# A four-layer graph and expert network on one core: 68 of 400 count scatters sent in two earlier stages, and the dense experts' bias rows weighted by VectorE

## The chip, the core and the metric

The kernel runs on one core of a Trainium2 chip. The metric is device time in microseconds (us) from the first to the last instruction of one execution; several executions are taken and the median is told.

## What is computed

The reference runs four layers, each a graph block and a feed-forward block, each on the layer-normed node features `x` (3125 nodes, 256 features) and each added back to `x`. There are 50000 edges with `src`, `dst` (sorted) and 64 edge features. Only two of the eight blocks matter here.

```python
# layer 0, feed-forward: 8 dense experts, all of them for every node
w   = softmax(xn @ Wr + br)                        # [3125, 8]
h1  = relu(scale1[e] * (xn @ W1[e]) + shift1[e])   # batch norm folded
h2  = relu(scale2[e] * (h1 @ W2[e]) + shift2[e])
x  += sum_e w[:, e] * (h2 @ Wo[e] + bo[e])
# layer 1, graph, three rounds of mean aggregation over the in-edges
h   = relu(mean_{edges into n} h[src] @ Wl + bl + h @ Wr + ...)
```

The bias row `bo[e]` enters each node as `sum_e w[n, e] * bo[e]`. The mean over in-edges is taken with a matrix of edge counts (node by node), which has to be built once from the list of edges.

## The kernel before

Nodes lie in 25 tiles of 128 rows, five tiles to a chunk (`CH`), 640 rows a chunk (`TOK`). The program is a sequence of stages. Each stage is a `Phase` with one `Block`: every engine (PE = TensorE, DVE = VectorE, ACT = ScalarE, POOL = GpSimd, SP = SyncE) runs its own hand-written list, with semaphores between them, and at the end all engines meet at a barrier. So the next stage starts when the slowest engine of the stage is through.

Around the change the stages are, in order:

- `edge_logits` (L692) of the first graph block. It gathers a row for each edge slot, and beside that writes zeros over the count matrix in DRAM (`counts`, L752, ACT's queue, semaphore `g.filled`) and works out on DVE, from all pairs of columns of the edge list, where each count goes (`put_at`) and how large it is (`put_n`).
- `segment_max` (L859): the maximum of the logits over each node's edges, by transposes on PE and four long scans on DVE. POOL has nothing here.
- `bulk`, then `edge_sum` (L576), in which POOL multiplies messages, then `bulk` again.
- `ffn0` (L1411): `node_rows` (L373) makes layer norm, the transposed rows `xt` and the router's logits; POOL has nothing here. `bulk` makes the softmax and folds the batch norms. `turn_weights` (L1166) transposes the router weights `w` into `wt`, 8 x 3200. `experts` (L1196) runs the dense experts.
- `gnn1` (L1724), whose first stage is `node_rows` again. Its last stage, `mean_layers` (L964), is the first that reads `counts`.

`experts` loops five times over the chunks. Within one iteration the order of the layers is fixed by a skewed list: expert e's first layer, expert e-1's second, expert e-2's output. Inner products go to `ps_h` (four buffers) and ACT makes the next hidden rows of them (L1307). Output products go to `ps_y` (four buffers); DVE multiplies each by the expert's weight, a column of `wc`, and adds it to `y` (L1325 for expert 0, L1327 for the others). After expert 7 come five more products a chunk, `wtc` (8 x 128, turned weights) with `b_out` (8 x 256), which are the weighted bias rows (L1280); DVE adds them with L1329. Then DVE adds `y` to `x` (L1333), and copies the next chunk's weights (L1316). PE may be four output products ahead of DVE:

```python
pe.wait_ge(added, i * NO + max(n - 3, 0))
```

Beside all this POOL sends the 400 scatters that put the counts into DRAM (L1244), one for each column of 125 edges, and lets at most 40 (`BK`) stand open before it waits for them. It first waits for `g.filled`. It waits for all 400 before the stage may end:

```python
pool.wait_ge(put, 16 * EC)
```

SP loads `b_out` and then the experts' weights, 24 loads of 256 KB; expert 0 starts when its three are there.

Of the kernel before, what the change touches and what calls it, by code (L numbers as in the profile page):

```python
# [6 lines left out]
ALU = mybir.AluOpType  # L7
ACT = mybir.ActivationFunctionType
# [31 lines left out]
BK = 40  # L40
CN = NT * P
# [312 lines left out]

def by_partition(ap):

    return ap.rearrange("(k p) c -> p k c", p=P)
# [15 lines left out]
def node_rows(nc, g, srcs, w_drams, cols, bias, sinks, ln=False, xn=None, xt=None, relu_add=None):  # L373
# [7 lines left out]
    with Phase(nc) as ph:  # L381
# [29 lines left out]
        with nc.Block() as block:  # L411
            @block.sync
# [446 lines left out]
def segment_max(nc, g, logits, maxima, H):  # L859
# [6 lines left out]
    with Phase(nc) as ph:  # L866
# [299 lines left out]
def turn_weights(nc, g, wts, wts_t):  # L1166

    with Phase(nc) as ph:
        fixed = ph.sb("fixed", [P, CH, NE], F32)
        ps_w = ph.ps("ps_w", [P, 2, 512])  # L1170
        laid, turned, taken = ph.sem("laid"), ph.sem("turned"), ph.sem("taken")
        with nc.Block() as block:
            @block.vector
            def _(dve):
                with nc.vector.Fori(0, NT // CH) as i:
                    dve.wait_ge(turned, i)
                    nc.vector.tensor_copy(fixed[:], wts[:, ds(i * CH, CH), :]).then_inc(laid, 1)

            @block.tensor
            def _(pe):  # L1180
                with nc.tensor.Fori(0, NT // CH) as i:
                    pe.wait_ge(laid, i + 1)
                    pe.wait_ge(taken, i * 2)
                    for j in range(CH):
                        ins = nc.tensor.transpose(ps_w[0:NE, j // 4, (j % 4) * P:(j % 4 + 1) * P], fixed[:, j, :], g.ident[:])
                    ins.then_inc(turned, 1)

            @block.scalar
            def _(act):
                with nc.scalar.Fori(0, NT // CH) as i:  # L1190
                    act.wait_ge(turned, i + 1)
                    nc.scalar.activation(wts_t[:, ds(i * TOK, 512)], ps_w[0:NE, 0, :], ACT.Copy).then_inc(taken, 1)
                    nc.scalar.activation(wts_t[:, ds(i * TOK + 512, P)], ps_w[0:NE, 1, 0:P], ACT.Copy).then_inc(taken, 1)


def experts(nc, g, xt, hidden, w_last, b_last, wts, wts_t):  # L1196
# [11 lines left out]
    outer = [(e, t) for e, l in order if l == L for t in range(CH)] + [(NE, t) for t in range(CH)]  # L1208
# [4 lines left out]
    with Phase(nc) as ph:  # L1213
# [3 lines left out]
        b_out = sb("b_out", [NE, D], F32)  # L1217
        wc = sb("wc", [P, CH, NE], F32)
        wtc = sb("wtc", [NE, TOK], F32)
# [4 lines left out]
        b_in, made, shaped, made_y, added, stored, wc_in, wt_in, put = (sem(x) for x in (  # L1224
            "b_in", "made", "shaped", "made_y", "added", "stored", "wc_in", "wt_in", "put"))
        with nc.Block() as block:
            @block.sync
            def _(sp):
                sp.dma_start(b_out[:], b_last).then_inc(b_in, 16)
# [7 lines left out]
            @block.gpsimd  # L1237
            def _(pool):
                pool.wait_ge(g.filled, 16 * ((NT + 1) * CH + ES))
                for b in range(EC // BK):  # L1240
                    if b:
                        pool.wait_ge(put, 16 * BK * b)
                    for j in range(b * BK, (b + 1) * BK):
                        nc.gpsimd.indirect_dma_start(  # L1244
                            out=g.counts, out_offset=bass.IndirectOffsetOnAxis(ap=g.put_at[:, j:j + 1], axis=0),
                            in_=g.put_n[:, j:j + 1], in_offset=None).then_inc(put, 16)
                pool.wait_ge(put, 16 * EC)

            @block.tensor
            def _(pe):  # L1250
                with nc.tensor.Fori(0, NT // CH) as i:
# [17 lines left out]
                    def outer_layer(e):  # L1269
                        if e < NE:  # L1270
                            pe.wait_ge(shaped, i * NI + done[(e, L - 1)])
                        else:
                            pe.wait_ge(wt_in, i + 1)
                            pe.wait_ge(b_in, 16)
                        for t in range(CH):
                            n = out_at[(e, t)]
                            pe.wait_ge(added, i * NO + max(n - 3, 0))
                            if e == NE:

                                ins = nc.tensor.matmul(ps_y[:, n % 4, 0:D], wtc[:, t * P:(t + 1) * P], b_out[:],  # L1280
                                                       start=True, stop=True)
                            else:
                                K = dims[L] // P
                                for k in range(K):
                                    ins = nc.tensor.matmul(ps_y[:, n % 4, 0:D], hid[L - 1][:, e % 2, k, t * P:(t + 1) * P],
                                                           ws[L][:, e, k, :], start=k == 0, stop=k == K - 1)
# [7 lines left out]
                    outer_layer(NE)  # L1294

            @block.scalar
            def _(act):
                with nc.scalar.Fori(0, NT // CH) as i:
                    act.wait_ge(made_y, i * NO)
# [1187 lines left out]
```

## Time and profile before

| | us |
|---|---|
| median of 3 runs | 7201.81 (7201.0 to 7206.65) |
| profiled execution, its own time | 7212.82 |
| its span, first to last instruction | 7211.0 |
| `segment_max` of the first graph block | 725.9 to 784.7 |
| `node_rows` of `ffn0` | 1069.7 to 1105.4 |
| `turn_weights` with both barriers | 1115.1 to 1127.8 |
| `experts`, to the next stage's first instruction | 1127.8 to 1763.7 |

Stages are given in us from the span's start. A row of the timeline has start, length, engine, line, operation, output <- input, and, in brackets, how long the engine was idle before it and what ended that. Rows that follow one another on an engine with the same names are merged (x5 are five instructions in one row). "SPq" is SP's queue of transfers, of which the row shows the issue and not the landing.

### The profile page before, as it was taken

How to read it: one execution, taken by the hardware profiler on the slowest of the kernel's cores; microseconds unless marked ns; L12 is line 12 of the kernel's file. 1: busy time of each engine (PE TensorE's matmuls, PEld its weight loads, DVE VectorE, ACT ScalarE, POOL GpSimd, SP SyncE). 2: the span in 40 equal slices, each digit the busy share in tenths (PEclk: the TensorE clock that was granted, in tenths of full speed). 3: DMA queues.
4: the chain of work that ended last, by engine and by line, in shares of the span. 5: the costliest groups of instructions: out<-in, count | busy, mean ns of one | idle time of the engine just before them, and what ended most of it. 6: DMA issues, size and time to landing. Idle time of an engine off the chain costs nothing. (4 is left out here: it accounts for less than half of the span.)

```text
span 7211.0 us, 90552 instructions
## 1 busy us (share of the span) xinstructions
PE 5064.2 (70%) x22571; PEld 4059.3 (56%) x22572; DVE 3026.6 (42%) x7105; ACT 1493.2 (21%) x3806; POOL 3390.5 (47%) x3180
## 2 busy tenths in 40 slices
PE   2877578995655487999994823329465886888466
PEld 2777456773344365888884723326354665766344
DVE  5655672222443472101011131137614775677453
ACT  1000563331000380000002310009231221222121
POOL 1777465775477480000003237748333776677100
PEclk8555788997877798999996955559687998899687
DMA  2999451001699563444544548857263886788100
GB/s 76 353 344 318 146 169 37 1 1 17 228 337 335 194 222 95 125 127 125 139 117 151 179 116 236 236 161 236 86 194 108 263 262 198 230 264 264 43 0 22
DMA packets 831975, 1217.80 MB, mean 169 GB/s; under 512 B 120484, under 2 KB 617741, under 8 KB 831785
## 3 DMA queue, kind: packets, MB, share of 16 engines
q1 hardware_dynamic: 386617, 514.07, 24.2%
q0 software_dynamic: 143680, 378.88, 18.0%
q10 hardware_dynamic: 301488, 322.74, 12.7%
q8 instruction: 67, 1.10, 0.1%
q14 instruction: 123, 1.01, 0.0%
HBM read 840.14 MB, written 374.71 MB: 168 GB/s over the span
## 5 line engine op out<-in xcount | busy, mean ns | idle before, releaser
L570 POOL DMA_INDIRECT logit_rows<-tab,src_a x832 | 824.7, 991 | 340.9 <-issue 229.0
L570 POOL DMA_INDIRECT max_rows<-tab,src_a x832 | 786.6, 945 | 382.4 <-issue 236.1
L689 PE MATMUL ps_a<-msg,sel 128*128 128x264 f32 (+2 forms) x2496 | 625.3, 399 | 124.3 <-DVEq L621 67.9
L1565 POOL DMA_INDIRECT moe_x<-xn,slot x100 | 97.2, 972 | 1218.3 <-POOLq L93 1188.4
L689 PEld LDWEIGHTS ps_a<-msg,sel 128*128 128x128 f32 x2496 | 453.4, 191 | 296.1 <-DVE acc L635 98.3
L1244 POOL DMA_INDIRECT counts<-put_n,put_at x400 | 476.6, 1192 | 251.1 <-issue 235.8
L1055 PE MATMUL ps_a<-hl,blocks 128*128 128x256 f32 x2600 | 578.0, 379 | 0.5 <-PE ps_a L1055 0.3
L1055 PEld LDWEIGHTS ps_a<-hl,blocks 128*128 128x128 f32 x2600 | 491.9, 190 | 78.1 <-issue 13.6
L570 POOL DMA_INDIRECT logit_rows<-tab_kv,src_a x416 | 397.6, 956 | 241.2 <-issue 117.7
L2004 DVE TENSOR_TENSOR_SCAN run<-same,run,ps_t 128x512 f32<-128x512 bf16 x416 | 508.4, 1265 | 0.9 <-PE ps_t L1932 0.9
L600 POOL TENSOR_TENSOR msg<-edge_rows,extra 128x1024 f32<-128x1024 f32 x208 | 393.4, 1904 | 200.6 <-DMA edge_rows<-slot_rows 126.0
L1923 PE MATMUL ps_e<-w,att 64*128 64x256 f32 x1664 | 467.2, 426 | 22.2 <-DMA att<-in_attr_t 22.2
L851 PE MATMUL ps_b<-q,sel_t 128*128 x832 | 303.0, 529 | 232.9 <-DVE sel_t L770 232.9
L851 PE MATMUL ps_b<-cols,sel_t 128*128 x832 | 194.4, 363 | 369.2 <-DVE sel_t L770 369.1
L1974 ACT ACTIVATE back<-ps_b 128x512 f32<-128x512 f32 x416 | 229.0, 595 | 850.0 <-PE ps_b L1941 822.0
L660 ACT ACTIVATE far<-lane,loc_a 128x128 f32<-128x128 f32 x1248 | 398.5, 390 | 16.9 <-PEq L93 6.9
L851 PEld LDWEIGHTS ps_b<-cols,sel_t 128*128 128x128 f32 x832 | 185.2, 328 | 378.7 <-issue 378.6
L1995 DVE TENSOR_TENSOR msg<-max_rows,ps_e 128x512 f32<-128x512 f32 x416 | 274.2, 685 | 292.3 <-DMA max_rows<-tab,src_a 184.5
L851 PEld LDWEIGHTS ps_b<-q,sel_t 128*128 128x128 f32 x832 | 209.7, 264 | 326.3 <-issue 288.3
L1121 DVE SCALAR_TENSOR_TENSOR new<-ps_a,rdeg,acc 128x256 f32<-128x256 f32 x75 | 36.2, 483 | 845.1 <-PE ps_a L1066 845.1
L1923 PEld LDWEIGHTS ps_e<-w,att 64*128 64x128 f32 x1664 | 327.1, 207 | 111.2 <-issue 60.3
L925 ACT ACTIVATE lt<-ps_x 128x512 f32<-128x512 f32 (+3 forms) x12 | 6.4, 552 | 1750.7 <-PE ps_x L899 1750.7
(439 smaller groups left out, 9409.0 us busy)
## 6 DMA issues: line engine op xcount, KB each, us to landing
slot_rows<-logit_rows ACTq DMA_DIRECT2D x312, 512.0 KB
edge_rows<-slot_rows SPq DMA_DIRECT2D x312, 512.0 KB
blocks<-counts SPq DMA_DIRECT2D x390, 320.0 KB
seg_rows<-back ACTq DMA_DIRECT2D x208, 512.0 KB
counts<-zeros ACTq DMA_DIRECT2D x130, 320.0 KB
locs<-loc_slots SPq DMA_DIRECT2D x312, 128.0 KB
att<-in_attr_t SPq DMA_DIRECT2D x1248, 32.0 KB
wf<-in_L_ffn_W SPq DMA_DIRECT2D x57, 512.0 KB
```

The lines of the kernel that those rows point to most:

```text
L570: self.nc.gpsimd.indirect_dma_start(out=self.rows[:, (n % Q) * Q + j, :], out_offset=None, in_=table, in_offset=bass.IndirectOffsetOnAxis( ...
L600: nc.gpsimd.tensor_tensor(msg[:, b % 2, :, 0:D].rearrange("p j (h d) -> p j h d", h=heads), ring.rows[:, b * Q:(b + 1) * Q, :].rearrange(" ...
L660: ins = nc.scalar.activation(far[:, n % 2, j, :], g.lane[:], ACT.Abs, scale=-1.0, bias=g.loc_a[:, n * Q + j:n * Q + j + 1])
L689: nc.tensor.matmul(ps_a[:, n % 8, 0:C], sel[:, b % 2, j, :], rhs, start=True, stop=True).then_inc(summed, 1)
L851: ins = nc.tensor.matmul(product(b, j), sel_t[:, b % 2, j, :], node_cols[:, ds(tiles[j], 1), :].rearrange("p a c -> p (a c)"), start=True, ...
L1055: ins = nc.tensor.matmul(ps_a[:, q % 2, 0:D], blocks[:, k % RC, n % CH, :], sides[l][:, n, :], start=n == 0, stop=i == 0 and n == NT - 1)
L1244: nc.gpsimd.indirect_dma_start(out=g.counts, out_offset=bass.IndirectOffsetOnAxis(ap=g.put_at[:, j:j + 1], axis=0), in_=g.put_n[:, j:j + 1 ...
L1565: nc.gpsimd.indirect_dma_start(out=g.moe_x, out_offset=bass.IndirectOffsetOnAxis(ap=slot[:, c, t:t + 1], axis=0), in_=xn[:, t, :], in_offs ...
L1923: ins = t.matmul(ps_e[:, k, j * D:(j + 1) * D], att[:, b * Q + 2 * k + j, :], w[:], start=True, stop=True)
L1974: a.activation(back[:, s:s + 2, :].rearrange("p j d -> p (j d)"), ps_b[:, k, :], ACT.Copy).then_inc(taken, 1)
L1995: v.tensor_tensor(msg[:, s:s + 2, :], ring.rows[:, s:s + 2, :], ps_e[:, k, :].rearrange("p (j d) -> p j d", j=2), ALU.add).then_inc(mixed, 1)
L2004: v.tensor_tensor_scan(run[:, b, c, :], same[:, b, :], ps_t[:, b % 2, c, :], run[:, (b - 1) % Q, c, GP - 1:GP], ALU.mult, ALU.max).then_in ...
```

## The change

1. The loop of scatters becomes a function `put_counts(nc, g, pool, lo, hi)` that sends columns lo to hi. `segment_max` of the first graph block sends 40 of them, `node_rows` of `ffn0` 28, `experts` the other 332. The wait for `g.filled` moves with the first, the wait for all 400 stays in `experts`. The semaphore is now one of the whole program.
2. `turn_weights` is gone, and with it `wt`, `wtc` and ACT's copy of `wtc` at the start of each iteration.
3. `b_out` now holds all eight bias rows on each of the 128 partitions (a broadcast load of 128 x 2048 in place of 8 x 256), and stands ahead of the weights on SP's queue as before. At the start of each iteration DVE builds `y` of the weighted bias rows: 5 `tensor_scalar`, then 35 `scalar_tensor_tensor`, all of them SBUF to SBUF. All output products are then added with `scalar_tensor_tensor`. The five bias products and five additions at the end of the iteration are gone.

```diff
+PUT0, PUT1 = 40, 68
+def put_counts(nc, g, pool, lo, hi):
+    if lo == 0:
+        pool.wait_ge(g.filled, 16 * ((NT + 1) * CH + ES))
+    for j in range(lo, hi):
+        if j and j % BK == 0:
+            pool.wait_ge(g.put, 16 * j)
+        nc.gpsimd.indirect_dma_start(
+            out=g.counts, out_offset=bass.IndirectOffsetOnAxis(ap=g.put_at[:, j:j + 1], axis=0),
+            in_=g.put_n[:, j:j + 1], in_offset=None).then_inc(g.put, 16)
+    if hi == EC:
+        pool.wait_ge(g.put, 16 * EC)
...
-def node_rows(nc, g, srcs, w_drams, cols, bias, sinks, ln=False, xn=None, xt=None, relu_add=None):
+def node_rows(nc, g, srcs, w_drams, cols, bias, sinks, ln=False, xn=None, xt=None, relu_add=None, puts=(0, 0)):
...
+            if puts[1]:
+                @block.gpsimd
+                def _(pool):
+                    put_counts(nc, g, pool, *puts)
...
-def segment_max(nc, g, logits, maxima, H):
+def segment_max(nc, g, logits, maxima, H, puts=(0, 0)):
...
+            if puts[1]:
+                @block.gpsimd
+                def _(pool):
+                    put_counts(nc, g, pool, *puts)
...
-def experts(nc, g, xt, hidden, w_last, b_last, wts, wts_t):
+def experts(nc, g, xt, hidden, w_last, b_last, wts):
...
-    outer = [(e, t) for e, l in order if l == L for t in range(CH)] + [(NE, t) for t in range(CH)]
+    outer = [(e, t) for e, l in order if l == L for t in range(CH)]
...
-        b_out = sb("b_out", [NE, D], F32)
+        b_out = sb("b_out", [P, NE, D], F32)
...
-                sp.dma_start(b_out[:], b_last).then_inc(b_in, 16)
+                sp.dma_start(b_out[:].rearrange("p e d -> p (e d)"), row_bc(b_last.rearrange("e d -> (e d)"))).then_inc(b_in, 16)
...
-                    for j in range(b * BK, (b + 1) * BK):
-                        nc.gpsimd.indirect_dma_start(
...
+                put_counts(nc, g, pool, PUT1, EC)
...
-                            if e == NE:
-                                ins = nc.tensor.matmul(ps_y[:, n % 4, 0:D], wtc[:, t * P:(t + 1) * P], b_out[:],
-                                                       start=True, stop=True)
...
-                    nc.scalar.activation(wtc[:], wts_t[:, ds(i * TOK, TOK)], ACT.Copy).then_inc(wt_in, 1)
...
+                dve.wait_ge(b_in, 16)
                 with nc.vector.Fori(0, NT // CH) as i:
...
+                    for e in range(NE):
+                        for t in range(CH):
+                            if e == 0:
+                                ins = v.tensor_scalar(y[:, t, :], b_out[:, 0, :], wc[:, t, 0:1], None, ALU.mult)
+                            else:
+                                dve.wait_ge(based, i * NO + e * CH + t - CH + 1)
+                                ins = v.scalar_tensor_tensor(y[:, t, :], b_out[:, e, :], wc[:, t, e:e + 1], y[:, t, :], ALU.mult, ALU.add)
+                            ins.then_inc(based, 1)
...
-            segment_max(nc, g, logits, maxima, 8)
+            segment_max(nc, g, logits, maxima, 8, puts=(0, PUT0))
...
+        node_rows(nc, g, [g.x], [(g.ins["L0_ffn_Wr"], 0, 0)], NE, g.ins["L0_ffn_br"], [(0, NE, w, None)], ln=True, xt=xt, puts=(PUT0, PUT1))
...
-        turn_weights(nc, g, w, wt)
```

The order on three engines shows it. On POOL, from the last gathers of the first `edge_logits` to the next `edge_logits`, before (`msg` is the messages of `edge_sum`, the ISA rows are the barriers):

```order
L570 DMA logit_rows<-tab,src_a 128x264 x416
L721 UNCONDITIONAL_BRANCH
L92 ISA x3
L592 UNCONDITIONAL_BRANCH
L600 TENSOR_TENSOR msg<-edge_rows,logits 128x4x256 x104
L591 UNCONDITIONAL_BRANCH
L92 ISA x5
L1237 UNCONDITIONAL_BRANCH
L1244 DMA counts<-put_n,put_at 10654720x1 x400
```

and now:

```order
L905 UNCONDITIONAL_BRANCH
L363 DMA counts<-put_n,put_at 10654720x1 x40
L903 UNCONDITIONAL_BRANCH
L93 ISA x2
L612 UNCONDITIONAL_BRANCH
L620 TENSOR_TENSOR msg<-edge_rows,logits 128x4x256 x104
L611 UNCONDITIONAL_BRANCH
L93 ISA x2
L428 UNCONDITIONAL_BRANCH
L363 DMA counts<-put_n,put_at 10654720x1 x28
L426 UNCONDITIONAL_BRANCH
L93 ISA x2
```

Forty scatters now stand ahead of the messages, 28 behind them, and one barrier fewer follows. The other 332 come after the last row shown.

On DVE, from `turn_weights` to the start of the experts' loop, before (`fixed` is a chunk of the router weights for the transpose):

```order
L1177 ISA
L1177 COPY fixed<-w 128x40
L1175 REGISTER_ALU
L1175 COMPARE_AND_BRANCH
L1172 UNCONDITIONAL_BRANCH
L1311 UNCONDITIONAL_BRANCH
L1314 UNCONDITIONAL_BRANCH
L1314 ISA
L1316 ISA
L1316 COPY wc<-w 128x40
L1317 REGISTER_ALU
L1320 REGISTER_ALU
```

and now:

```order
L1285 UNCONDITIONAL_BRANCH
L1289 UNCONDITIONAL_BRANCH
L1289 ISA
L1291 ISA
L1291 COPY wc<-w 128x40
L1292 REGISTER_ALU
L1297 TENSOR_SCALAR y<-b_out,wc 128x256 x5
L1299 REGISTER_ALU
L1300 SCALAR_TENSOR_TENSOR y<-b_out,wc,y 128x256
L1299 REGISTER_ALU
```

Between the copy of the weights and the first output product there now stand 40 instructions, the last 35 with a register instruction ahead of each, since the value waited for depends on the loop's counter.

On PE, the end of the experts' loop, before:

```order
L1285 MATMUL ps_y<-w_8062,hid_8064 128x256 x2
L1273 REGISTER_ALU
L1277 REGISTER_ALU
L1280 MATMUL ps_y<-b_out,wtc 128x256
L1277 REGISTER_ALU
L1280 MATMUL ps_y<-b_out,wtc 128x256
```

and now:

```order
L1262 MATMUL ps_y<-w_8039,hid_8041 128x256 x2
L1237 REGISTER_ALU
L1237 COMPARE_AND_BRANCH
L1220 UNCONDITIONAL_BRANCH
L498 UNCONDITIONAL_BRANCH
```

The loop now turns straight behind expert 7's last output product.

## Rows read from the trace of the kernel before

**Rows 1.** Busy time by stage: us, PE, PEld, DVE, ACT, POOL, PEclk, DMA share, GB/s

```profile
725.50:785.40 59.90, 12.73 (x58) 11.34 (x58) 39.74 (x14) 8.91 (x33) 0.00 (x0) 0.54 0.09 14
1069.60:1106.00 36.40, 31.19 (x150) 29.44 (x150) 23.87 (x110) 10.59 (x31) 0.00 (x0) 0.50 0.01 1
1127.70:1684.00 556.30, 540.76 (x2130) 407.53 (x2130) 115.27 (x235) 201.27 (x325) 418.67 (x352) 0.98 0.11 13
1684.00:1763.60 79.60, 0.00 (x0) 0.00 (x0) 0.00 (x0) 0.00 (x0) 57.96 (x49) 0.50 0.07 1
```

**Rows 2.** Timeline, the end of the experts and the first load of gnn1

```profile
1682.23 1.49 DVE L1333 TENSOR_TENSOR x<-x,y 128x1280 f32 x1
...
1758.90 1.19 POOL L1244 DMA_INDIRECT counts<-put_n,put_at  x1 [0.30 <-issue]
1763.67 0.37 SPq L415 DMA_DIRECT2D w<-in_L_gnn_Wq  x1
```

**Rows 3.** The scatters by their line: min/median/max ns, first and last start

```profile
L1244 POOL DMA_INDIRECT counts<-put_n,put_at x400: 1182/1187/2426, 1128.7 to 1758.9; - x134
```

**Rows 4.** Timeline, the first segment maximum

```profile
725.97 1.89 DVE L939 COPY lp<-logits 128x3328 f32<-128x3328 f32 x1 [3.31 <-PEq L93]
...
779.33 5.39 ACT L932 ACTIVATE maxima<-ps_x 128x128 f32<-128x128 f32 x26 [45.18 <-PE ps_x L916]
```

**Rows 5.** Timeline, node rows, batch norms folded, and the transitions between

```profile
1069.70 0.40 SPq L415 DMA_DIRECT2D w<-in_L_ffn_Wr  x1
...
1105.27 0.17 DVE L462 TENSOR_TENSOR w<-ps_o,brow 128x8 f32<-128x8 f32 x1 [0.69 <-PE ps_o L507]
1106.17 0.80 SPq L1141 DMA_DIRECT2D vec<-in_L_ffn_vec  x2
...
1114.95 0.17 DVE L1431 TENSOR_TENSOR vec<-vec 128x16 f32<-128x16 f32 x1
```

**Rows 6.** Timeline, the start of the experts

```profile
1127.82 0.29 SPq L1229 DMA_DIRECT2D b_out<-in_L_ffn_bo  x1
...
1128.65 1.25 POOL L1244 DMA_INDIRECT counts<-put_n,put_at  x1 [96.29 <-issue]
...
1133.02 7.63 PE L1265 MATMUL ps_h<-xt,w 128*128 x16 [6.73 <-DMA w<-in_L_ffn_Wo]
```

**Rows 7.** Transfers of all queues, 1127.8 to 1150

```profile
DMA packets 6926, 6.32 MB, mean 285 GB/s; under 512 B 800, under 2 KB 6924, under 8 KB 6924
```

**Rows 8.** Timeline, where the experts' loop turns to chunk 3 and to chunk 4

```profile
1461.35 2.42 PE L1280 MATMUL ps_y<-b_out,wtc 8*128 8x256 f32 x10
1463.70 4.58 PE L1265 MATMUL ps_h<-xt,w 128*128 x16
1464.38 1.56 DVE L1333 TENSOR_TENSOR x<-x,y 128x1280 f32 x1
1477.77 4.48 PE L1285 MATMUL ps_y<-w,hid 128*128 128x256 f32 x20
...
1571.78 6.26 PE L1265 MATMUL ps_h<-xt,w 128*128 x16
```

**Rows 9.** Timeline of VectorE: node rows, edge_sum's additions, the routed experts' pairs

```profile
1072.67 1.71 DVE L450 TENSOR_SCALAR rows<-x,mv,rstd 128x256 f32<-128x256 f32 x5
...
905.99 0.43 DVE L635 TENSOR_TENSOR odd<-odd,ps_a 128x264 f32 x1
906.35 0.43 DVE L635 TENSOR_TENSOR acc<-acc,ps_a 128x264 f32 x1
906.79 0.43 DVE L635 TENSOR_TENSOR odd<-odd,ps_a 128x264 f32 x1
...
4122.38 1.00 DVE L1720 SCALAR_TENSOR_TENSOR x<-back,w,x 128x256 f32<-128x256 f32 x2 [7.13 <-DMA back<-moe_y,slot]
```

**Rows 10.** Gathers by line, 170 to 720 with the pair work, and 1900 to 2700

```profile
L570 POOL DMA_INDIRECT logit_rows<-tab,src_a x410 | 422.7, 1031 | 124.9 <-issue 113.3 <-DMA slot_rows<-logit_rows 7.3 <-DVE logits L792 4.3
L570 POOL DMA_INDIRECT logit_rows<-tab_kv,src_a x395 | 377.4, 955 | 122.4 <-issue 111.6 <-DMA slot_rows<-logit_rows 10.5 <-DVE logits L784 0.3
```

More of the change, by code:

```diff
@@ L1163, in _ @@
                         make(nc.scalar).then_inc(turn, 1)
[L1166 to L1193, printed above, removed]
-def experts(nc, g, xt, hidden, w_last, b_last, wts, wts_t):
+def experts(nc, g, xt, hidden, w_last, b_last, wts):
     L = len(hidden)
@@ L1216, in experts @@
         hid = [sb(f"hid{l}", [P, 2, dims[l + 1] // P, TOK], F32) for l in range(L)]
-        b_out = sb("b_out", [NE, D], F32)
+        b_out = sb("b_out", [P, NE, D], F32)
         wc = sb("wc", [P, CH, NE], F32)
-        wtc = sb("wtc", [NE, TOK], F32)
         y = sb("y", [P, CH, D], F32)
@@ L1223, in experts @@
         w_in = [sem(f"w_in{e}") for e in range(NE)]
-        b_in, made, shaped, made_y, added, stored, wc_in, wt_in, put = (sem(x) for x in (
-            "b_in", "made", "shaped", "made_y", "added", "stored", "wc_in", "wt_in", "put"))
+        b_in, made, shaped, made_y, added, stored, wc_in, based = (sem(x) for x in (
+            "b_in", "made", "shaped", "made_y", "added", "stored", "wc_in", "based"))
         with nc.Block() as block:
@@ L1238, in _ @@
             def _(pool):
[L1239 to L1242, printed above, removed]
-                    for j in range(b * BK, (b + 1) * BK):
-                        nc.gpsimd.indirect_dma_start(
-                            out=g.counts, out_offset=bass.IndirectOffsetOnAxis(ap=g.put_at[:, j:j + 1], axis=0),
-                            in_=g.put_n[:, j:j + 1], in_offset=None).then_inc(put, 16)
-                pool.wait_ge(put, 16 * EC)
+                put_counts(nc, g, pool, PUT1, EC)
             @block.tensor
@@ L1269, in outer_layer @@
                     def outer_layer(e):
[L1270 to L1274, printed above, removed]
+                        pe.wait_ge(shaped, i * NI + done[(e, L - 1)])
                         for t in range(CH):
@@ L1277, in outer_layer @@
                             pe.wait_ge(added, i * NO + max(n - 3, 0))
-                            if e == NE:
-                                ins = nc.tensor.matmul(ps_y[:, n % 4, 0:D], wtc[:, t * P:(t + 1) * P], b_out[:],
-                                                       start=True, stop=True)
[L1282 to L1286, printed above, removed]
+                            K = dims[L] // P
+                            for k in range(K):
+                                ins = nc.tensor.matmul(ps_y[:, n % 4, 0:D], hid[L - 1][:, e % 2, k, t * P:(t + 1) * P],
+                                                       ws[L][:, e, k, :], start=k == 0, stop=k == K - 1)
                             ins.then_inc(made_y, 1)
@@ L1293, in _ @@
                             outer_layer(e)
-                    outer_layer(NE)
             @block.scalar
@@ L1322, in _ @@
                             dve.wait_ge(added, i * NO + out_at[(e - 1, t)] + 1)
-                        src = ps_y[:, n % 4, 0:D]
-                        if e == 0:
-                            ins = v.tensor_scalar(y[:, t, :], src, wc[:, t, e:e + 1], None, ALU.mult)
-                        elif e < NE:
-                            ins = v.scalar_tensor_tensor(y[:, t, :], src, wc[:, t, e:e + 1], y[:, t, :], ALU.mult, ALU.add)
-                        else:
-                            ins = v.tensor_tensor(y[:, t, :], src, y[:, t, :], ALU.add)
+                        else:
+                            dve.wait_ge(based, i * NO + NO - CH + t + 1)
+                        ins = v.scalar_tensor_tensor(y[:, t, :], ps_y[:, n % 4, 0:D], wc[:, t, e:e + 1], y[:, t, :], ALU.mult, ALU.add)
                         ins.then_inc(added, 1)
@@ L1416, in ffn0 @@
         w = sb("w", [P, NT, NE], F32)
-        wt = sb("wt", [NE, NP_], F32)
         top, tot = sb("top", [P, NT], F32), sb("tot", [P, NT], F32)
         vec = [sb(f"vec{q}", [P, 5, NE, KD], F32) for q in range(2)]
-        node_rows(nc, g, [g.x], [(g.ins["L0_ffn_Wr"], 0, 0)], NE, g.ins["L0_ffn_br"], [(0, NE, w, None)], ln=True, xt=xt)
+        node_rows(nc, g, [g.x], [(g.ins["L0_ffn_Wr"], 0, 0)], NE, g.ins["L0_ffn_br"], [(0, NE, w, None)], ln=True, xt=xt, puts=(PUT0, PUT1))
         steps = softmax8(w[:], top[:], tot[:])
@@ L1432, in ffn0 @@
         bulk(nc, steps, loads=[(vec[q][:], (g.ins["L0_ffn_vec1"], g.ins["L0_ffn_vec2"])[q]) for q in range(2)])
-        turn_weights(nc, g, w, wt)
         experts(nc, g, xt, [(g.ins["L0_ffn_W1"], ACT.Relu, vec[0][:, 1, :, :], vec[0][:, 0, :, :]),
                             (g.ins["L0_ffn_W2"], ACT.Relu, vec[1][:, 1, :, :], vec[1][:, 0, :, :])],
-                g.ins["L0_ffn_Wo"], g.ins["L0_ffn_bo"], w, wt)
+                g.ins["L0_ffn_Wo"], g.ins["L0_ffn_bo"], w)
 def top2(nc, g, w, oh, oh2, w0, w1, bias_rows=()):
@@ L2430, in build @@
         g.filled = nc.alloc_semaphore("filled")
+        g.put = nc.alloc_semaphore("put")
         edge_steps(nc, g)
```

1 line of the change is left out of this document (removed).

## The prediction

> **What bounds the kernel now.** Stages end at a barrier, so I read the chip stage by stage and asked of each which engine is last. First the busy times by stage: in the experts' stage PE is busy 541 of 556 us at nearly full clock, and then for 80 us only POOL works [rows 1]. The timeline at the end says what that tail is. VectorE's last addition ends at 1682.23 + 1.49 = 1683.7, POOL's last scatter starts at 1758.90 and the next stage's first load goes out at 1763.67 [rows 2]. So POOL, not PE, ends this stage, 80 us late. The scatters by their line: 400 of them, median 1.187 us, first start 1128.65, last 1758.90 [rows 3, 6]. With 0.30 us of issue between them [rows 2] the plain pace is 1.49 us; the whole block goes at 630.2 / 399 = 1.58 us, which has the waits after every 40 and odd gaps in it. POOL is idle in the segment maximum and in the node rows before the experts [rows 1]: that is where the change puts 68 scatters.
>
> **Part by part.** The sum is made against the profiled execution, 7212.8 us, which is 11.0 over the median of the runs.
>
> *Segment maximum, 40 scatters.* In the experts POOL starts 0.8 us after SP; here the stage begins at 725.9 [rows 4], so POOL starts at about 726.6. The last scatter ends at 726.6 + 39 x 1.49 + 1.19 = 785.9 at the plain pace and 789.4 at 1.58. ScalarE ends the stage today at 779.33 + 5.39 = 784.7 [rows 4]. POOL does not wait for landings here. So the stage grows by 1.2 to 4.7 us; I take **+3**, the middle.
>
> *Node rows, 28 scatters.* Start 1069.70 + 0.8 = 1070.5, end 1111.9 (plain) to 1114.4 (at 1.58), against 1105.27 + 0.17 = 1105.4 today [rows 5]. Its cover is too short by 6.5 to 9.0 us; I take **+7.5**. The wait at column 40 is for scatters sent 300 us before and costs nothing.
>
> *turn_weights.* From the last batch-norm instruction's end, 1115.1, to SP's first load in the experts, 1127.82, are 12.7 us; a plain change of stage costs 1106.17 - 1105.4 = 0.7 [rows 5, 6]. So **-12.0**, all of it on the path.
>
> *The experts, POOL.* 332 scatters at 1.58: 0.8 + 331 x 1.58 + 1.2, and 2.6 until the last has landed, is 528 us from SP's first load.
>
> *The experts, PE and VectorE.* Today 1683.7 - 1127.8 = 555.9 us.
> - Bias products: from their first to the next iteration's first product 1463.70 - 1461.35 = 2.35 us, five times (the last one through VectorE's additions): -11.8 [rows 8].
> - The broadcast of b_out is 1.05 MB ahead of expert 0's weights on SP's queue; at the 285 GB/s of this stretch [rows 7] that is 3.7 us, less the 0.35 the small load takes: +3.4. Nothing hides it, PE waits for these weights already, 6.7 us [rows 6]. Bounds 2 and 5.
> - VectorE's 40 new instructions. Let T0 be where PE starts an iteration. The addition to x starts 0.68 after T0 today [rows 8]; without the five additions ahead of it (0.43 each, by edge_sum's [rows 9]) and with T0 2.35 earlier it starts at T0 + 0.9, and with the copy of wc the bias rows begin at T0 + 2.65. The five tensor_scalar go at 0.34 (five of L450 take 1.71 us [rows 9]). For the 35 others no row shows the same operation in a row with a waited register. Nearest are edge_sum's additions, whose starts are 0.36 and 0.44 apart [rows 9]; the floor is 0.34, the ceiling the routed experts' dependent pairs, 0.52 apart (1.00 for two of 0.485) [rows 9]. I take 0.42: 1.7 + 14.7 = 16.4 us, ready at T0 + 19.0, first output product added at T0 + 19.5. PE's output products begin at 1477.77 - 1463.70 = T0 + 14.1 five tiles of rows take 4.48, and the fifth, which needs that addition, is due at T0 + 17.6 [rows 8]. So PE stands about 2 us an iteration, four times; in the first one VectorE has the time of the weight loads to spare. +8.
> - But in three of four turns today the first 16 products behind those with 8 rows take 6.26 us and not 4.58 [rows 8]. Either that goes with the 8-row products, or the 1.7 us falls into VectorE's delay; both ways 3 x 1.7 = -5.
> - ScalarE's copy of wtc hid behind PE: 0. Together 555.9 - 11.8 + 3.4 + 8 - 5 = 550.5 us to VectorE's end, over POOL's 528, so **PE with VectorE now ends the stage**, with 22 us to spare. Plus 0.7 for the change of stage, against 1763.67 - 1127.82 = 635.85: **-84.6**.
>
> The sum is 3 + 7.5 - 12.0 - 84.6 = **-86 us**. Against the median: 7201.8 - 86 = **7116 us**. What follows (gnn1 to the end) moves as a whole; the counts are read only in gnn1's last stage.
>
> **Bounds.** Low end: 1.2 + 6.5 - 12, and no stand of PE at a pace of 0.34, b_out 2 us: 635.85 - (555.9 - 11.8 + 2 - 5 + 0.7) = 94; in all -98, 7104. High end: 4.7 + 9 - 12, and at 0.52 the bias rows end at T0 + 22.5, PE stands 5.5 us four times, b_out 5: 635.85 - (555.9 - 11.8 + 5 + 22 - 5 + 0.7) = 69; in all -67, 7135. The runs spread over 6 us; with that 7098 to 7138.
>
> **A rule weighed.** Do VectorE's instructions hold up POOL's scatters? The row that bears on it is the gather: 1031 ns beside the pair work, whose VectorE instructions read two SBUF tensors, 955 ns later on [rows 10]. That is 0.08 us on each; scatters at 1.66 end the two early stages at +8 and +11, 9 more than taken, and take 0.8 + 331 x 1.66 + 3.8 = 554 us in the experts, 4 more than PE. That is 7129, inside the range. The Trainium skill ("SBUF — State Buffer", Who interferes with whom) is stricter in one case: a copy or tensor_scalar from SBUF to SBUF in VectorE's two-port mode takes the port pair that POOL needs to write a transfer's descriptors, and POOL stands for the whole instruction. By that rule the new places are bad ones, for node rows are full of tensor_scalar.
>
> **Rivals.**
> 1. *POOL stands for every such instruction.* In node rows 25 L450 at 0.34 us hold it 8.5 us, in the segment maximum the copy 1.9 [rows 4, 9]; in the experts 25 x 0.34 = 8.5 us go into the 22 to spare. That gives -86 + 10 = -76, 7126. It is the mechanism of the rule above. For it: the copy of 3328 numbers takes 1.89 us, 0.57 ns each, so a doubled mode exists here. Against it: L450 takes 0.34 us for 256, 1.3 ns each, so it is not in that mode. 8%.
> 2. *POOL still ends the experts.* From 1.65 us a scatter on it does. If the 0.08 of the gathers doubles on a scatter, 1.74: 331 x 1.74 + 5.3 = 581, so -54.6, with +11 and +13 earlier and -12 that is -43: 7159. For it: VectorE now works twice as much beside the scatters. Against: median 1187 and minimum 1182 lie together, though 235 VectorE instructions ran beside them [rows 1, 3]. 5%.
> 3. *Slower than before: a scatter stands while VectorE is busy at all.* VectorE is busy 39.7 us in the segment maximum and 23.9 in node rows [rows 1], 115 - 11 + 200 x 0.42 = 188 in the experts: +43, +31, -12 and 528 + 188 + 0.7 - 635.85 = +81, in all +143, 7345. It decides from 1.85 us a scatter, where the sum of the four stages is nil. Against it: the same median and minimum, and gathers only 0.08 us longer beside a VectorE busy most of the time. 3%.
>
> That the scatters are not spread as meant is excluded by the order on POOL, 40, 28 and 332. For what I haven't seen (a clock that falls, a fetch of code) 2% remain on the good side.
>
> **How the numbers follow.** Forecast 82%, rival 1 8%, rival 2 5%, rival 3 3%, rest 2%. The range of 7098 to 7138 takes in the forecast and rival 1. A measurement can tell about 0.2%, 14 us. Only rival 3 is over it on the slow side: slower 3%, within 1%, faster 96%.
>
> **What would show it.** In the changed kernel: POOL last in the segment maximum by some 3 us and in node rows by 7.5; no stage between the folding of the norms and the experts; scatters of 1.19 us in all three places; in the experts VectorE's addition to x last, some 550 us after SP's load, POOL done 20 us before; between iterations no products of 8 rows, and a wait of PE for `y` of about 2 us at the fifth output product. It would be wrong if POOL were last in the experts, if the 35 instructions went over 0.52 us apart, or if scatters beside VectorE took over 1.3 us.

## The result and the profile after

The change is faster by 0.4%, a third of what was forecast. Before takes 7206.0 us (7201.0 to 7221.0, six runs), the changed kernel 7177.9 us (7174.9 to 7182.0, six runs): ratio 0.9959, 95% interval 0.9946 to 0.9972, 28 us. The forecast was 7116 us with a range that ended at 7138, so the time lies outside it.

The profiled execution of the changed kernel took 7180.7 us (span 7178.7, clock 0.797; before 0.795). Busy time by stage, each from SP's first load to that of the next stage; columns as in [rows 1]:

```profile
723.95:821.39 97.44, 12.08 (x58) 10.85 (x58) 43.37 (x15) 13.06 (x35) 72.73 (x40) 0.54 0.10 10
1097.52:1143.06 45.54, 31.19 (x150) 29.43 (x150) 25.54 (x110) 10.58 (x31) 33.25 (x28) 0.50 0.08 2
1152.70:1740.98 588.28, 522.77 (x2080) 394.90 (x2080) 181.69 (x410) 197.47 (x320) 454.62 (x332) 0.96 0.11 14
```

These are the segment maximum (with the short `bulk` stage behind it), the node rows and the experts. POOL has 72.7 us of busy time on 40 scatters in the first, 1.82 us each; 28 in the second at 1.19; 332 in the third at 1.37.

| stage | before | after | difference | forecast |
|---|---|---|---|---|
| segment maximum | 67.3 | 97.4 | +30.1 | +3 |
| node rows | 36.5 | 45.5 | +9.1 | +7.5 |
| norms folded, turned weights | 21.7 | 9.6 | -12.0 | -12.0 |
| experts | 635.9 | 588.3 | -47.6 | -84.6 |
| sum | | | -20.4 | -86 |

The scatters by line, after, where [rows 3] had 2426 ns as the longest:

```profile
L363 POOL DMA_INDIRECT counts<-put_n,put_at x400: 1182/1187/12369, 724.8 to 1735.4; - x134
```

The median has not moved, but one scatter took 12.4 us. The timeline of the segment maximum shows the first kind of long scatter:

```profile
743.67 1.19 POOL L363 DMA_INDIRECT counts<-put_n,put_at  x1 [0.30 <-issue]
744.75 7.08 DVE L970 TENSOR_TENSOR_SCAN fwd<-cut,lt 128x3328 f32<-128x3328 bf16 x1
745.17 7.66 POOL L363 DMA_INDIRECT counts<-put_n,put_at  x1 [0.30 <-issue]
751.75 7.07 DVE L971 TENSOR_TENSOR_SCAN bwd<-cut,lt 128x3328 f32<-128x3328 bf16 x1
753.13 6.67 POOL L363 DMA_INDIRECT counts<-put_n,put_at  x1 [0.30 <-issue]
...
762.77 7.15 DVE L985 TENSOR_TENSOR_SCAN fwd<-cut,start,lt 128x3328 f32<-128x3328 bf16 x1
763.10 7.82 POOL L363 DMA_INDIRECT counts<-put_n,put_at  x1 [0.30 <-issue]
769.95 7.15 DVE L986 TENSOR_TENSOR_SCAN bwd<-cut,start,fwd 128x3328 f32<-128x3328 bf16 x1
771.22 6.88 POOL L363 DMA_INDIRECT counts<-put_n,put_at  x1 [0.30 <-issue]
```

Four scatters meet the four long scans, and each ends 1.0 us after its scan ends: 744.75 + 7.08 = 751.83, and 745.17 + 7.66 = 752.83. Together they take 29.0 us where four cost 4.8: 24.3 us of the 30. The second scan begins at 751.75, before the first has ended, and still the first scatter gets through between the two. The second kind of long scatter stands in the experts, at the start of a turn:

```profile
1158.21 1.82 DVE L1297 TENSOR_SCALAR y<-b_out,wc 128x256 f32<-128x256 f32 x5
1159.44 1.19 POOL L363 DMA_INDIRECT counts<-put_n,put_at  x1 [0.30 <-issue]
1159.95 13.93 DVE L1300 SCALAR_TENSOR_TENSOR y<-b_out,wc,y 128x256 f32<-128x256 f32 x35
1160.94 1.34 POOL L363 DMA_INDIRECT counts<-put_n,put_at  x1 [0.30 <-issue]
1162.58 12.36 POOL L363 DMA_INDIRECT counts<-put_n,put_at  x1 [0.30 <-issue]
1175.25 1.19 POOL L363 DMA_INDIRECT counts<-put_n,put_at  x1 [0.30 <-issue]
```

The chain of 35 new instructions ends at 1173.88, the scatter at 1174.94. Each of the five turns has one such scatter, 5 x 11.2 = 56 us. So POOL still ends the experts, and VectorE is done 43 us before the next stage starts:

```profile
1696.14 1.49 DVE L1312 TENSOR_TENSOR x<-x,y 128x1280 f32 x1
1741.02 1.73 DVE L455 BATCH_NORM_STATS2 stats<-x 128x6 f32<-128x256 f32 x5 [43.39 <-PEq L94]
```

The second row is VectorE's first instruction of the next stage. VectorE's last addition ends 544.9 us after the stage's first load. What TensorE waited for in that stage (us in total, times, longest):

```profile
PE ps_h L1251 <- DMA w<-in_L_ffn_Wo: 27.4, 1, 27.4
PE ps_y L1262 <- DVE y L1308: 4.0, 4, 1.0
```

### The profile page after: what moved, and what is told of

Read it like the earlier page. It is cut to its first block and busy times, and to the rows that moved or that the text cites. A ratio compares the mean times of both kernels' runs of the same rounds, so it can differ in the third digit from the quotient of the medians.

```text
span 7178.7 us, 90370 instructions
## 1 busy us (share of the span) xinstructions
PE 5043.3 (70%) x22496; PEld 4041.0 (56%) x22497; DVE 3098.8 (43%) x7275; ACT 1490.2 (21%) x3791; POOL 3476.9 (48%) x3180
## 5 line engine op out<-in xcount | busy, mean ns | idle before, releaser
L363 POOL DMA_INDIRECT counts<-put_n,put_at x400 | 560.6, 1402 | 212.2 <-issue 137.2
```

Of the source, the lines that this page charges most:

```text
L363: nc.gpsimd.indirect_dma_start(out=g.counts, out_offset=bass.IndirectOffsetOnAxis(ap=g.put_at[:, j:j + 1], axis=0), in_=g.put_n[:, j:j + 1 ...
```

## The experiments

The theory at the start: a scatter makes no progress while VectorE runs an instruction that reads two SBUF tiles. The chips that ran these kernels differ: before took 7891 us on the chip of kernels 1 to 4, 7865 us on that of 5 to 8, and 7216 us on that of 9 to 12. Each ratio is against before on the same chip. The stages studied here take nearly the same time on all of them (with 40 scatters the segment maximum took 96.5 to 97.8 us, with 28 the node rows 45.5 to 45.8 and once 47.0), so their times are compared across chips. Sums by stage are against the traced stages of before.

**1. All scatters in the experts.** Constants only; the new bias rows stay.

```diff
-PUT0, PUT1 = 40, 68
+PUT0, PUT1 = 0, 0
```

> All 400 scatters back in the experts, the bias rows still weighted by VectorE. Theory (a scatter stands through VectorE's chain of scalar_tensor_tensor with two SBUF inputs, L1300): one scatter of about 12.4 us in each of the five turns, 5 x 11.2 = 56 us and some 5 us beside the additions into x, so the experts take 635.9 + 61 = 697 us, the bulk work before them 12 us less, and the kernel is slower than before by about 49 us (some 7255 us). Rival (the 61 us have another cause, such as the order in which the scatters were cut): no scatter over 3 us, experts 636 us, about 7194 us.

Ratio 1.0053 (1.0036 to 1.0070), +42 us. Segment maximum 66.7, experts 695.5 us. The five long scatters are there again, in each turn one:

```profile
1363.10 12.37 POOL L363 DMA_INDIRECT counts<-put_n,put_at  x1 [0.30 <-issue]
1469.90 12.38 POOL L363 DMA_INDIRECT counts<-put_n,put_at  x1 [0.31 <-issue]
1576.70 12.37 POOL L363 DMA_INDIRECT counts<-put_n,put_at  x1 [0.30 <-issue]
```

VectorE's bias rows alone make the kernel slower than before, though they relieve TensorE: its time was not what the stage waited for.

**2. None in the segment maximum.** `PUT0, PUT1 = 0, 28`.

> No scatter in the segment maximum, 28 in the node rows, 372 in the experts. Theory (the scans' scatters cost the 30 us in the segment maximum, and in the experts a scatter beyond the 332 costs 1.58 us): segment maximum 67.3 us as before, node rows 45.5 us, experts 588.3 + 40 x 1.58 = 651.5 us, so about +13 us against before, some 7219 us. Rival (the stage's 30 us come from something else than the scatters, such as its place or its neighbours): segment maximum still over 90 us.

Ratio 1.0008 (0.9998 to 1.0018). Segment maximum 67.0, node rows 45.8, experts 650.5 us. Without scatters the stage has its old length, and 40 more in the experts cost 62.2 us, 1.56 each. Putting them into the segment maximum for 30 us was still a gain, of half the size meant.

**3. The split kept, the bias undone.** Before with the split scatters, turned weights and 8-row products.

```diff
-                pool.wait_ge(g.filled, 16 * ((NT + 1) * CH + ES))
-                for b in range(EC // BK):
...
-                pool.wait_ge(put, 16 * EC)
+                put_counts(nc, g, pool, PUT1, EC)
```

> The scatters split as in the change (40, 28, 332), the bias rows by TensorE from turned weights as before the change. Theory: segment maximum +30 us and node rows +9 us as in the change; in the experts no scatter over 3 us, POOL's 332 are done after some 528 us, TensorE and VectorE end them at about 557 us (-79 us); sum about -40 us, some 7166 us, and so 12 us better than the change. Rival (scatters are held by VectorE's other work in the experts too, or by their DMAs): experts near 588 us as in the change, about 7205 us.

Ratio 0.9946 (0.9929 to 0.9963). Experts 554.4 us, no scatter over 2.5 us in them, mean 1197 ns. TensorE and VectorE end the stage. By stages that is -43 us, where the whole change has -20: without its other half, the split would be worth more than the two together.

**4. Bias rows added into PSUM.**

```diff
-                        ins = v.scalar_tensor_tensor(y[:, t, :], b_out[:, e, :], wc[:, t, e:e + 1], y[:, t, :], ALU.mult, ALU.add)
...
+                        v.tensor_tensor(src, src, b_out[:, e, :], ALU.add).then_inc(based, 1)
+                        dve.wait_ge(based, i * NO + n + 1)
```

> The change, with the bias row added by VectorE into the product in PSUM (tensor_tensor, one input from PSUM) before the row is weighted, so that no scalar_tensor_tensor reads two SBUF tiles; VectorE has 200 instructions of about 0.35 us where the chain had 200 of 0.4 us. Theory: no scatter of 12.4 us, POOL done after 528 us, experts about 547 us (-88 us), segment maximum +30, node rows +9, bulk work -12: sum about -60 us, some 7146 us. Rival (any work of VectorE on the bias rows holds a scatter, whatever its inputs): the scatters are held as long as before in sum, experts about 588 us, 7178 us.

Ratio 0.9910 (0.9893 to 0.9927). Experts 542.9 us. POOL over that stage:

```profile
L363 POOL DMA_INDIRECT counts<-put_n,put_at x332 | 395.4, 1191 | 146.1 <-issue 115.1 <-DMA counts<-put_n,put_at 17.3 <-POOLq L94 13.8
```

Mean 1191 ns instead of 1369. With the chain gone the stage is as long as the prediction had it (551.2), less the 8 us of waits that the chain would have caused.

**5. Thirteen in the segment maximum.** `PUT0, PUT1 = 13, 41`.

> The change with 13 scatters instead of 40 in the segment maximum (they are out before VectorE's first scan), 28 in the node rows, 359 in the experts. Theory (only scatters that meet the scans cost there, and the stage's end is not POOL's): segment maximum 67 to 68 us as before, node rows 45.5 us, experts 588.3 + 27 x 1.58 = 631 us, sum about -8 us against before (ratio 0.999). Rival (any scatter in the stage costs, because they share queues or a barrier with its loads): segment maximum over 75 us.

Ratio 0.9978 (0.9969 to 0.9988). Segment maximum 67.9, node rows 47.0, experts 627.1 us. Thirteen scatters, all out before the first scan, cost the stage 0.9 us against kernel 2. What costs there is meeting the scans.

**6. The chain spread.** The rows of expert e's bias just ahead of the five outputs of expert e.

```diff
                     for e in range(NE):
                         for t in range(CH):
...
-                                dve.wait_ge(based, i * NO + e * CH + t - CH + 1)
+                                dve.wait_ge(added, i * NO + out_at[(e - 1, t)] + 1)
...
+                        for t in range(CH):
+                            n = out_at[(e, t)]
```

> The change, with VectorE's weighted bias rows no longer in one chain of 40 at a turn's start, but five ahead of each expert's five outputs; the same instructions with two SBUF tiles. Theory (a scatter makes no progress while such an instruction runs, so what counts is their sum): no scatter of 12 us, but 35 groups a kernel in which one scatter takes about 3 us; POOL ends the experts, at about 588 to 600 us, no gain over the change. Rival (a group of 2 us slips between or is caught up): experts at 543 to 550 us, ended by TensorE, some 40 us better than the change.

Ratio 0.9905 (0.9889 to 0.9922): this is what the rival expected, and the first form of the theory falls. Experts 540.7 us, with the same 175 instructions on the same tiles. One group of five and the scatters beside it:

```profile
1409.31 2.06 DVE L1300 SCALAR_TENSOR_TENSOR y<-b_out,wc,y 128x256 f32<-128x256 f32 x5
1409.64 1.20 POOL L363 DMA_INDIRECT counts<-put_n,put_at  x1 [0.30 <-issue]
1411.15 1.27 POOL L363 DMA_INDIRECT counts<-put_n,put_at  x1 [0.30 <-issue]
```

The first scatter lies wholly inside the group and is not held. So what counts is not the sum of such instructions, but how long they follow each other.

**7. A version that places the scatters by what was learnt.** Bias as in 4; scatters 0, 20, 320, and 60 in gnn1's node rows, where POOL is idle for 109 us.

```diff
-PUT0, PUT1 = 40, 68
+PUT0, PUT1, PUT2 = 0, 20, 340
...
-                put_counts(nc, g, pool, PUT1, EC)
+                put_counts(nc, g, pool, PUT1, PUT2)
...
-                          ln=True)
+                          ln=True, puts=(PUT2, EC))
```

> Bias rows added into PSUM as in bias_in_psum; no scatter in the segment maximum, 20 in the node rows before the experts, 320 in the experts, the last 60 in the node rows of the next layer (109 us in which POOL has nothing to do). Theory: segment maximum +0, node rows +0 (20 x 1.49 + 1.1 + 2.2 for the landing = 33 us of 36.5), bulk work -12, experts 543 us (-93), next node rows +0: sum -105 us against before, ratio 0.9867 where before takes 7890 us. Rival (the next layer's node rows are slowed by scatters beside their table stores and 1024-column products): that stage 5 to 30 us longer, sum -75 to -100 us.

Ratio 0.9851 (0.9834 to 0.9867), 117 us. Segment maximum 66.8, node rows 37.1, experts 541.8, gnn1's node rows 109.8 us (before 108.8).

**8. Chains with gaps, one kind at a time.** Version 4 plus instructions on an unread tile, each waiting for the one just before it.

```diff
+                chains = [[ts] * 14, [tt] * 14, [stt] * 14, [scan] * 10, [copy] * 14, [stt, ts] * 7, [stats] * 14, []]
...
+                    for make in chains[e]:
+                        dve.wait_ge(probed, i * total + n + 1)
+                        make().then_inc(probed, 1)
```

> bias_in_psum, with chains of one kind of VectorE instruction on a tile that nobody reads, behind the outputs of seven of the eight experts in each turn (128x256 f32, SBUF to SBUF): 14 tensor_scalar, 14 tensor_tensor of two tiles, 14 scalar_tensor_tensor of two tiles, 10 tensor_tensor_scan of two tiles, 14 copies, scalar_tensor_tensor and tensor_scalar by turns (7 each), 14 bn_stats. Theory A (two SBUF inputs hold a scatter): scatters take as long as the chain for tensor_tensor, scalar_tensor_tensor and scan (5 to 7 us), 1.2 us beside tensor_scalar, copy and bn_stats; beside the mixed chain one or two of 1.6 us and more. Theory B (only scan and scalar_tensor_tensor hold, tensor_tensor does not): 1.2 us beside tensor_tensor too. Theory C (any chain without a gap holds, whatever its inputs): all seven about as long as their chains.

None of the three theories came out. This kernel and kernel 11 were executed once each, so only their traces are used. Experts 542.6 us. The longest scatters of that stage, 2.0 and 2.2 us, stand beside additions to x; beside the chains none in five turns took over 1.62 us. The short scans, and the same scalar_tensor_tensor that hold a scatter 11 us in the change, let the scatters by (two of the chains, and one scatter beside the second):

```profile
1437.82 7.29 DVE L1294 SCALAR_TENSOR_TENSOR junk<-b_out 128x256 f32<-128x256 f32 x14
1450.75 7.21 DVE L1295 TENSOR_TENSOR_SCAN junk<-b_out 128x256 f32<-128x256 f32 x10
1450.94 1.48 POOL L363 DMA_INDIRECT counts<-put_n,put_at  x1 [0.30 <-issue]
```

One thing differs besides length: here 14 take 7.29 us, 0.52 apart with 0.49 each, so there is a gap between them. In the change 35 of 0.47 take 13.93, 0.396 apart: the next begins before the last has ended. That gave theory D: a scatter is held by one long instruction, or by a run of them without a gap.

**9. The change again**, on the chip of the last four.

> The change itself, unedited, for the chip on which the experiments run. All theories: segment maximum 97.5 us, node rows 45.5 us, experts 588 us with five scatters of 12.4 us; the ratio to before that its first comparison gave, 0.996.

Ratio 0.9961 (0.9948 to 0.9973). Segment maximum 97.4, node rows 45.6, experts 588.3 us.

**10. One gap behind each instruction of the chain.** The sharpest test, one line of the change:

```diff
-                                dve.wait_ge(based, i * NO + e * CH + t - CH + 1)
+                                dve.wait_ge(based, i * NO + e * CH + t)
```

> The change with one edit: each of the 35 scalar_tensor_tensor of a turn's chain waits for the one just before it (as in the probe, where the pace was 0.52 us instead of 0.396), not for the one five before. Theory D (a scatter is held by one instruction with two SBUF tiles until it ends, and by a run of them only where they follow each other without a gap): no scatter over 3 us though VectorE runs the same 175 instructions and the chain is longer (18 us), POOL done after some 530 us, TensorE waits for VectorE in each turn, experts 550 to 570 us. Theory A (the sum of such instructions holds): scatters of 16 us, experts 600 us and more.

Ratio 0.9940 (0.9923 to 0.9956). POOL in the experts, and what TensorE waited for:

```profile
L363 POOL DMA_INDIRECT counts<-put_n,put_at x332 | 398.9, 1202 | 146.2 <-issue 115.0 <-DMA counts<-put_n,put_at 17.3 <-POOLq L94 13.9
PE ps_y L1262 <- DVE y L1308: 21.5, 4, 5.4
```

The longest scatter in this stage takes 1.72 us, not 12.4. The chain is 4.3 us longer (18.19), TensorE waits 5.4 us a turn, and the stage still falls from 588.3 to 569.2 us. Theory D holds for the chain. The scans fit it only in part: their second begins 0.08 us before the first has ended, like the chain's instructions, and yet a scatter gets through between them.

**11. Chains without a gap.** As 8, but on five tiles, each instruction waiting for the one four or five before it.

```diff
+                chains = [[ts] * 20, [tt] * 20, [stt] * 20, [copy] * 20, [stt] * 10, [stt] * 20, [stt, ts] * 10, []]
...
+                        gap = k == 0 or (e == 5 and k % 5 == 0)
+                        dve.wait_ge(probed, i * total + n + (1 if gap else 1 - min(k, 4)))
```

> bias_in_psum with other chains behind the experts' outputs, on five tiles that nobody reads, each instruction waiting for the one five before it (so without a gap, as in the change): 20 tensor_scalar, 20 tensor_tensor, 20 scalar_tensor_tensor, 20 copies, 10 scalar_tensor_tensor, 20 scalar_tensor_tensor with a gap after each fifth, scalar_tensor_tensor and tensor_scalar by turns (10 each). Theory D: scatters of 5 to 7 us to the chain's end beside 20 tensor_tensor and 20 scalar_tensor_tensor, some 3 us beside 10, at most 2.5 us beside the chain with gaps; 1.2 us beside tensor_scalar and copy; in the mixed chain under 2 us. Rival E (in the change the scatter was held by something else than the missing gap, such as its length of 14 us): no scatter over 2 us beside any of the seven.

The third turn, chain by chain, with the longest scatter beside each:

```profile
1395.05 6.22 DVE L1292 TENSOR_SCALAR junk<-b_out 128x256 f32<-128x256 f32 x20
1397.41 1.20 POOL L363 DMA_INDIRECT counts<-put_n,put_at  x1 [0.31 <-issue]
1407.98 6.79 DVE L1293 TENSOR_TENSOR junk<-b_out 128x256 f32<-128x256 f32 x20
1411.10 4.72 POOL L363 DMA_INDIRECT counts<-put_n,put_at  x1 [0.30 <-issue]
1420.96 8.01 DVE L1294 SCALAR_TENSOR_TENSOR junk<-b_out 128x256 f32<-128x256 f32 x20
1425.19 4.84 POOL L363 DMA_INDIRECT counts<-put_n,put_at  x1 [0.30 <-issue]
1433.84 5.13 DVE L1295 COPY junk<-b_out 128x256 f32<-128x256 f32 x20
1437.03 1.25 POOL L363 DMA_INDIRECT counts<-put_n,put_at  x1 [0.30 <-issue]
1446.77 4.07 DVE L1294 SCALAR_TENSOR_TENSOR junk<-b_out 128x256 f32<-128x256 f32 x10
1450.62 1.28 POOL L363 DMA_INDIRECT counts<-put_n,put_at  x1 [0.30 <-issue]
1459.70 8.37 DVE L1294 SCALAR_TENSOR_TENSOR junk<-b_out 128x256 f32<-128x256 f32 x20
1462.72 1.41 POOL L363 DMA_INDIRECT counts<-put_n,put_at  x1 [0.30 <-issue]
```

Twenty tensor_tensor hold a scatter in each of the five turns (4.1 to 5.1 us), twenty scalar_tensor_tensor too (3.4 to 5.6). The same twenty with a gap after each fifth (the last pair of rows) hold none. Ten without a gap hold none for over 1.7 us, where I had expected 3: in three turns the scatter that began 3.4 us into the run of 4.04 ended 1.1 us after it, so it was held too, but had only 0.6 us to lose. Copies and the mixed chain hold none. Tensor_scalar held none in four turns, but one for 4.8 us in the second turn (chain from 1288.45, scatter at 1290.04); that one is not explained. Theory D had expected 1.2 us there.

**12. Spread bias rows and scatters placed as in 7.**

> The bias rows as in spread (five ahead of each expert's outputs), the scatters placed as in best (0 in the segment maximum, 20 in the node rows, 320 in the experts, 60 in the next layer's node rows). Segment maximum +0, node rows +0.6, bulk work -12, experts 541 us (-95), next node rows +1: -105 us against before, as best, ratio 0.985 to 0.987. Rival (spread's scatters cost where the weights come in at the start): up to 3 us more.

Ratio 0.9841 (0.9825 to 0.9858), 7099.3 against 7216.2 us, the lowest ratio of all, though kernel 7's interval overlaps it. Its stages:

```profile
726.16:793.18 67.02, 12.52 (x58) 11.12 (x58) 43.38 (x15) 13.15 (x35) 0.00 (x0) 0.55 0.08 13
...
1116.20:1657.54 541.34, 522.45 (x2080) 395.67 (x2080) 182.52 (x410) 197.49 (x320) 386.37 (x320) 0.99 0.11 15
1657.54:1767.52 109.98, 94.29 (x250) 43.30 (x250) 57.47 (x185) 9.83 (x30) 71.19 (x60) 0.94 0.29 75
```

By stages that is -105 us, as expected. The ratio gives -115 (-126 to -102).

## Why the prediction was wrong

**"PE with VectorE now ends the stage, with 22 us to spare"** failed. It assumed 1.58 us for each of the 332 scatters, whatever VectorE ran beside them. Five took 12.4 us, and others beside the addition to x up to 2.4, so POOL needed some 60 us more than the 528 it had been given. Two of the prediction's three signs of being wrong came: POOL last in the experts, and scatters beside VectorE of over 1.3 us. Kernels 4, 6 and 10 take the holding away in three ways (another operation, another place, a gap) and the scatters fall back to a mean of 1.19 to 1.21 us. This one step is 37 of the 66 us missing in the sum.

**Segment maximum, "+3, the middle" of 1.2 to 4.7** failed for the same reason. The scans held four scatters for 24.3 us. Of the other 5.8 us, 4.4 lie inside the forecast's bounds; 1.4 is the longer end of the stage (below). Kernels 2 and 5 show that the stage keeps its length without that meeting.

**Node rows, +7.5,** came out as +9.1. POOL's last scatter ended 42.3 us after the start, the plain pace exactly. The rest is the end of the stage, of which the prediction said "POOL does not wait for landings here". The stage's end:

```profile
1138.60 1.18 POOL L363 DMA_INDIRECT counts<-put_n,put_at  x1 [0.31 <-issue]
1143.06 0.80 SPq L1166 DMA_DIRECT2D vec<-in_L_ffn_vec  x2
```

3.3 us lie between its end and the next load, where the same stage, ended by VectorE, had 0.7 [rows 5]. A landing comes 2.6 us after a scatter's start, here at 1141.2. A stage's end that waits for it and then takes its 0.7 us gives 1141.9, so about 1.2 us of the 3.3 have another cause. In the segment maximum the last scatter starts at 810.26 and the next stage's first instruction at 813.62, 0.8 us after a landing, which fits such a wait. All this was read from the rows, not tested; what the end waits for is open.

**Turned weights, -12.0:** measured -12.0. **The sum for TensorE and VectorE, 550.5 us:** measured 544.9, and 539.6 to 541.8 in kernels 4 and 6, where the chain was gone. Pace of the chain 0.396 for the 0.42 taken, TensorE's wait 1.0 us a turn for 2, which is 4 of the 5.6 us. The broadcast of b_out made PE's start 3.0 us later for 3.4 (8.2 us after the first load, 5.2 before). All of this was near, and none of it set the time.

**"A rule weighed"** used the wrong row. The gathers' 1031 against 955 ns [rows 10] stand beside instructions with two SBUF inputs that do follow without a gap, but in short runs, here from 303.71 to 306.02:

```profile
303.71 0.52 DVE L798 TENSOR_TENSOR equal<-place 125x349 f32<-125x349 f32 x1
304.14 0.20 DVE L802 TENSOR_TENSOR put_n<-put_n,equal 125x50 f32<-125x50 f32 x1
```

Kernel 6 shows that runs of 2.1 us hold no scatter, and kernel 11 that scatters get through in the first 2.6 us of a longer one. The step from short runs to one of 13.9 us was the error.

The Trainium skill's rule on copies and tensor_scalar, which the prediction cited, has one row for it, the first scatter of the segment maximum:

```profile
723.99 1.89 DVE L964 COPY lp<-logits 128x3328 f32<-128x3328 f32 x1 [3.46 <-PEq L94]
724.77 2.20 POOL L363 DMA_INDIRECT counts<-put_n,put_at  x1 [10.18 <-POOLq L94]
```

It ends 1.1 us after the copy, the sign of a held scatter, and takes 2.20 us in every kernel that sends scatters there; it costs 1.0 us, and no kernel tested it alone. The rule is not borne out by node rows, where scatters beside L470 took 1.18 to 1.19 us, so rival 1's 8.5 us there did not come, nor by the copies of kernel 11 (1.25 us). Beside tensor_scalar the one scatter of 4.8 us in kernel 11 is the only hint of it. That scatter and the one beside the copy are both the first after a pause on POOL (2.40 and 10.18 us); whether this matters was not tested.

The same section of the Trainium skill ("SBUF — State Buffer", Who interferes with whom) also says that a VectorE instruction with two SBUF inputs contends with a GpSimd instruction that reads SBUF. The long scans and the chains without gaps agree with that, if the scatter counts as such an instruction: its offsets and its values stand in SBUF tiles (`put_at`, `put_n`). It also notes, marked as an inference, that tensor_tensor leaves descriptor generation alone. Twenty tensor_tensor held a scatter for 4.1 to 5.1 us here, so that note can't be relied on for this scatter; which of its parts is held no run shows.

**Rival 3** ended on the slower side and had the mechanism near its right form: "a scatter stands while VectorE is busy". I argued it away with the median and the minimum, which can't show five events in 400. The maximum could: the row said 2426 [rows 3]. Before's timeline has that scatter beside an addition of two SBUF tiles:

```profile
1572.46 1.49 DVE L1333 TENSOR_TENSOR x<-x,y 128x1280 f32 x1
1572.59 2.43 POOL L1244 DMA_INDIRECT counts<-put_n,put_at  x1 [0.30 <-issue]
```

It ends 1.07 us after the addition, the same sign as behind the scans. And the scans stood in before's segment maximum in plain sight; the prediction named only the copy there:

```profile
745.77 7.08 DVE L945 TENSOR_TENSOR_SCAN fwd<-cut,lt 128x3328 f32<-128x3328 bf16 x1
```

Open: the stages of the change sum to -20, its ratio gives -28 us, and most of the other kernels also come out some 5 to 12 us better than their stages. That lies within the intervals, if at their edge. Which stage it would belong to was not found: the part behind the experts took 5447 us in the trace of before, 5438 and 5441 in the two of the change, and 5452 in that of kernel 10.

## What to carry to other kernels

Before work is moved beside other work, list the long or gapless instructions of the place it is moved to, and look at the longest durations of the moved instruction beside anything like them: a median hides a few long ones. If two engines get in each other's way, a different place, a gap, or another operand may remove it: with the five rows ahead of each expert's outputs instead of 35 in one chain, the same instructions cost 48 us less. And when an engine has a fixed amount to issue, give each stage what fits under what ends it, landing included (20 here, not 28), and look for a stage further on where it is idle.

## What the runs showed of the hardware

- An indirect transfer issued by GpSimd (125 elements, 1.19 us) stands while VectorE runs one long scan of two SBUF tiles, and ends 1.0 us after it: 6.7 to 7.8 us beside scans of 7.1.
- It also stands through a run of tensor_tensor or scalar_tensor_tensor on two SBUF tiles in which the next begins before the last has ended (scalar_tensor_tensor: 0.396 us apart, 0.472 long). The one or two scatters that begin in the first 2.6 us of the run get through in 1.2 to 1.4 us; the next, which began 2.6 to 5.6 us into the run, stands to its end. In runs of 2.1 us and of 4 us no scatter took over 1.7 us. Why the first get through is open, and so is why one gets through between two long scans that overlap by 0.08 us.
- A scatter beside one copy of 128x3328 f32 (1.89 us) took 2.20 us and ended 1.1 us after the copy; beside 20 copies of 128x256 without a gap it took 1.25 us.
- A wait on the instruction just before costs 0.12 us each (0.52 apart for 0.396), and lifts the hold.
- VectorE's scans take 7.07 to 7.15 us with and without scatters beside them. It is delayed a little elsewhere: five tensor_scalar of the node rows took 1.89 to 2.07 us beside scatters, 1.71 without [rows 9].
